# Second layer computed unturned, with a float16 feed-forward and its ELU split between ScalarE and VectorE

## The reference, cut to what matters

```
h = elu(_gat_heads(enc_inputs, adj, W_heads, a_heads))      # layer 1, four heads
h = transpose(h, (0, 2, 1, 3)).reshape(B, N, -1)
out = _gat_heads(h, adj, W_out[None], a_out[None])[:, 0]     # layer 2
out = elu(out)
ffn = maximum(out @ w1 + b1, 0.0) @ w2 + b2
y = ffn + out
return (y - mean(y)) / sqrt(var(y) + LN_EPS) * ln_gamma + ln_beta
```

## Time and profile before

| | |
|---|---|
| median of 3 runs | 1723.54 us (1720.91 to 1724.05) |
| span of the profiled execution | 1722.6 us |
| TensorE busy | 1584.4 us, 92% |
| VectorE busy | 1452.3 us, 84% |
| ScalarE busy | 1382.1 us, 80% |
| GpSimd busy | 1004.7 us, 58% |
| DMA moved | 242.45 MB, mean 141 GB/s |

### The profile page before, as it was taken

The page is one execution under the profiler, slowest core; times in us unless marked ns, Lnnn a source line. Parts: engine busy times, 40 slices in busy tenths (PEclk is TensorE's granted clock), DMA queues, the critical chain, the costliest instruction groups (busy, mean ns, idle before and its releaser), DMA issues.

```text
span 1722.6 us, 36184 instructions
## 1 busy us (share of the span) xinstructions
PE 1584.4 (92%) x13119; PEld 1319.3 (77%) x13120; DVE 1452.3 (84%) x2520; ACT 1382.1 (80%) x1858; POOL 1004.7 (58%) x1425
## 2 busy tenths in 40 slices
PE   5548999999999999999999999999999999999965
PEld 3336878788787887788887887888777888888854
DVE  5877699879998899979999799988999798898583
ACT  4177499879988799878997799878997799999660
POOL 4064367447575566656575566656666475675271
PEclk9769999999999999999999999999999999999988
DMA  8266499749986698678977699868976698798572
GB/s 262 57 147 115 94 190 162 120 95 189 174 151 117 123 187 164 118 122 160 189 141 117 113 184 178 137 98 152 190 156 112 104 172 172 129 133 147 101 118 36
DMA packets 780882, 242.45 MB, mean 141 GB/s; under 512 B 746368, under 2 KB 774016, under 8 KB 780576
## 3 DMA queue, kind: packets, MB, share of 16 engines
q1 hardware_dynamic: 771744, 231.70, 72.1%
q0 software_dynamic: 8960, 8.42, 4.3%
HBM read 38.54 MB, written 16.94 MB: 32 GB/s over the span
## 4 chain that ended last, share of the span: by engine, by line
PE 49%; DVE 18%; ACT 13%; issue 10%; DMA 5%; POOL 3%; SPq 1%; DVEq 0%; ACTq 0%; POOLq 0%
PE ps L129 11%; PE ps L1260 7%; PE ps L1261 7%; PE ps L1266 7%; DVE p_lo L1041 5%; PE ps L138 5%; PE ps L1280 4%; PE ps L1293 3%; ACT p_hi L925 3%; ACT xr L912 3%; DVE xr L1034 3%; PE ps L1341 2%; DMA cat<-f_rows 2%; ACT xr L918 2%; DVE ht_lo L1066 2%
## 5 line engine op out<-in xcount | busy, mean ns | idle before, releaser
L1260 PE MATMUL ps<-pt_hi,hv_hi 128*128 128x256 f16 x2048 | 463.8, 274 | 26.4 <-DMA pt_hi<-p_hi 26.4
L1261 PE MATMUL ps<-pt_hi,hv_lo 128*128 128x256 f16 x2048 | 463.7, 274 | 0.0
L1041 DVE SCALAR_TENSOR_TENSOR p_lo<-xr,rden,p_hi 128x1024 f16<-128x1024 f32 x320 | 409.6, 1280 | 30.4 <-ACT p_hi L925 30.4
L925 ACT ACTIVATE p_hi<-xr,rden 128x1024 f16<-128x1024 f32 x320 | 365.4, 1142 | 32.8 <-POOL rden L849 32.8
L847 POOL TENSOR_SCALAR den<-sums 128x1 f32<-128x1 f32 x320 | 156.4, 489 | 363.2 <-ACT xr L918 361.2
L918 ACT ACTIVATE xr<-xr,shift 128x1024 f32<-128x1024 f32 x320 | 365.5, 1142 | 2.4 <-POOL shift L862 2.4
L1034 DVE CUSTOM_DVE_ANT_0 xr<-cat,mask_add 128x1024 f32<-128x1024 f32 x256 | 311.2, 1217 | 7.5 <-DMA cat<-f_rows 7.5
L912 ACT ACTIVATE xr<-xr,f1h 128x1024 f32<-128x1024 f32 x256 | 292.6, 1143 | 5.5 <-DVE mx L1034 5.5
L849 POOL TENSOR_TENSOR rden<-den,minus_one 128x1 f32<-128x1 f32 x320 | 268.3, 838 | 26.7
L860 POOL TENSOR_SCALAR zt<-mx,f1h 128x1 f32<-128x1 f32 x256 | 197.6, 772 | 120.0 <-DVE mx L1034 117.1
L1266 PE MATMUL ps<-pt_lo,hv_hi 128*128 128x256 f16 x2048 | 266.3, 273 | 0.9 <-DMA pt_lo<-p_lo 0.9
(11 more groups left out here) (192 smaller groups left out, 3193.3 us busy)
## 6 DMA issues: line engine op xcount, KB each, us to landing
cat<-f_rows SPq DMA_DIRECT2D x32, 512.0 KB, 4.6
out<-xx SPq DMA_DIRECT2D x32, 256.0 KB, 2.4
xx<-in_x SPq DMA_DIRECT2D x28, 256.0 KB, 3.3
out<-fin POOLq DMA_DIRECT2D x28, 256.0 KB, 5.3
pt_hi<-p_hi SPq DMA_TRANSPOSE x320, 3.3
pt_lo<-p_lo SPq DMA_TRANSPOSE x320, 3.3
adj_i<-in_adj SPq DMA_DIRECT2D x4, 1024.0 KB, 11.7
f2o<-f2o_rows SPq DMA_DIRECT2D x8, 512.0 KB, 4.4
```

The source lines that it names most:

```text
L925: nc.scalar.activation(p_hi[:, k % P_SLOTS, :], xr[:, k % X_SLOTS, :], ACT.Copy, scale=rden[:, k % 8:k % 8 + 1]).then_inc(hi_done, 1)
L1041: nc.vector.scalar_tensor_tensor(p_lo[:, k % P_SLOTS, :], xr[:, k % X_SLOTS, :], rden[:, k % 8:k % 8 + 1], p_hi[:, k % P_SLOTS, :], ALU.mu ...
L1260: nc.tensor.matmul(to, vh, hi, start=t == 0, stop=False)
L1261: nc.tensor.matmul(to, vl, hi, start=False, stop=False)
```

## The change

1. **Layer 2 unturned.** In `attend` of a layer-2 pair the turned probabilities are now the stationary operand and the values move, so the output has tokens on partitions. It is still 48 matmuls of 256 columns. The waits are by unit: the matmuls of the first unit start when its own transposes have landed.
2. **ELU of layer 2.** ScalarE does the exponential (`elu_exp`) and then, after `softmax` of the same step, a second operation `elu_below`: maximum of 0 and C - C e, in place, with scale and bias from columns of `sc`. VectorE has one operation left: maximum(x, 0) minus that. The min-and-add operation on VectorE goes for layer 2.
3. **Float16 feed-forward.** `o2_high` (ScalarE, step n-5) and `o2_low` (VectorE, n-6) split the ELU output of each pair into float16 halves of 128 x 512; SyncE's queue turns both (`turn_o2`, n-6) into `hs_hi` and `hs_lo`, shared with the first layer's tasks. `ff1` uses three float16 products per block (12 matmuls of 512 columns per half batch) in place of four float32 matmuls of 512 columns.
4. **Residual and b2.** The ELU output is already in token order, so the identity matmuls go; one bfloat16 matmul per tile adds b2 (`b2_rows`), and `y_out` adds the residual in the same single operation over 1024 columns.
5. **Steps.** `CLOSING` and `LAST` change, part of `STEADY` moves by one step, `GAP` goes from 6 to 8.
6. **Start.** w1 is scaled and split, b2 is split into three bfloat16 rows on GpSimd, with one more norm product.

Cut to its core:

```diff
-        GAP = 6
+        GAP = 8
...
-                      turn_h0_0=-38, turn_h0_1=-34, m0=-31, m1=-30, m2=-29, m3=-28, mj_high0=-31, mj_high1=-29, mj_high2=-28, mj_high3=-27,
...
+                      turn_h0_0=-37, turn_h0_1=-33, m0=-30, m1=-29, m2=-28, m3=-27, mj_high0=-30, mj_high1=-28, mj_high2=-27, mj_high3=-26,
...
-        CLOSING = dict(ff1_0=-1, ff2_0=2, ff1_1=4, ff2_1=6, hidden_0=1, hidden_1=5, y_0=4, y_1=9, save_f2o=-22, load_f2o=-16)
...
+        CLOSING = dict(ff1_0=2, ff2_0=4, ff1_1=6, ff2_1=8, hidden_0=3, hidden_1=7, y_0=5, y_1=9, save_f2o=-22, load_f2o=-16)
...
+            def turn_o2(j):
...
+                cols = slice(i // 4 * N + i % 4 * F, i // 4 * N + (i % 4 + 2) * F)
+                for whole, part, ready in ((hs_hi, o2_hi[:, c % 2, :], o2hi_done), (hs_lo, o2_lo[:, :], o2lo_done)):
+                    sp.wait_ge(ready, c + 1)
+                    sp.dma_start_transpose(whole[:, cols].rearrange("p (t i) -> p t i", i=P), part).then_inc(o2_T[c % 2], DMA)
...
+            def elu_below(j):
+
+                act.wait_ge(e2_done, count2(j) + 1)
+                e = eq[:, j % 2, :, :].rearrange("p k n -> p (k n)")
+                nc.scalar.activation(e, e, ACT.Relu, bias=scale(S_OREC), scale=scale(S_ONEG)).then_inc(exp_done, 1)
...
+            def o2_high(j):
...
+                nc.scalar.activation(o2_hi[:, c % 2, :], o2_of(j), ACT.Copy, scale=2.0 ** -P_LOG).then_inc(o2hi_done, 1)
...
+                    nc.vector.scalar_tensor_tensor(o2_of(j).rearrange("p (k n) -> p k n", k=KF), x, 0.0, e, ALU.max, ALU.subtract).then_inc(elu_done, 1)
...
+                if layer == 2:
+                    for u in range(2):
+                        to = psA[:, (j % 2) * 512 + u * F:(j % 2) * 512 + (u + 1) * F]
+                        pe.wait_ge(hi_T[slot + u], turn)
...
+                for slot in range(2):
+                    pe.wait_ge(o2_T[slot], (2 * p + i + 1) * 2 * DMA)
...
-                    for k in range(KF):
-                        last = nc.tensor.matmul(to[:, t * F + k * P:t * F + (k + 1) * P], o2T_of(p, i)[:, k, tok], ident[:, :], start=False, stop=k == KF - 1)
+                    last = nc.tensor.matmul(to[:, t * F:(t + 1) * F], pick[:, :], b2_rows[:, :], start=False, stop=True)
```

More of the change, by code:

```diff
@@ L158, in scores_T @@
                 for t in range(T):
[L159 removed]
+                    last = nc.tensor.transpose(to[:, t * NF:(t + 1) * NF], rows[:, t * P:(t + 1) * P], ident8[0:NF, 0:NF])
                 return last
@@ L995, in _ @@
                     softmax(unit_at(n + 3))
+                j = pair_at(n - ELU_EXP + 2)
+                if j is not None and kinds[2 * j][0] == 2:
+                    elu_below(j)
                 if unit_at(n + 2) is not None:
@@ L1003, in _ @@
                     ht_high(j)
+                j = pair_at(n - O2_HIGH)
+                if j is not None and kinds[2 * j][0] == 2:
+                    o2_high(j)
                 for s in range(B):
@@ L1187, in _ @@
                     ht_low(j)
+                j = pair_at(n - O2_LOW)
+                if j is not None and kinds[2 * j][0] == 2:
+                    o2_low(j)
                 for s in range(B):
```

148 lines of the change are left out of this document (109 added, 39 removed).

## The result

The changed kernel takes 1784.14 us (median of 4, 1782.91 to 1786.41) against 1723.8 us for the kernel before on the same chip: ratio 1.0353, 95% interval [1.0338, 1.0367]. It is 60 us slower, where 1727.7 was forecast with a range that ended at 1750. Slower was the likeliest of the three outcomes that the prediction gave (0.53), but by 4 us, little more than the 3.4 us that it could tell from no change; the size was missed by far.

A forecast was written before the change was run, and what follows sets the result against it. TensorE was taken to bound layer-1 units, taking turns with ScalarE in layer-2 stretches. Stretches +11.4, end -7.5, start +0.3 gave +4.2 on 1722.6, plus 0.9 to the median: 1727.7 us; own bounds 1718 to 1736, 8-in-10 range 1703 to 1750.

The forecast's parts named there:

- What TensorE saves: In `ff1` and `ff2`: 4.4 us per batch, 35 us over eight batches, if TensorE were the only bound.
- What ScalarE gets: Layer-2 stretch: `elu_below` and `o2_high` add 0.6 us each, 1.2 per pair and 4.8 per stretch.
- What VectorE gets: Per layer-2 pair: a 0.42 us operation goes, a 0.75 us one comes; +0.3, or 10 us in all, mostly beside waits.
- Rival B: Layer-2 stretch: longer ELU chain holds VectorE, ScalarE waits for its masked row; 3 to 4 us more per stretch, 1747; chance 0.20.
- SyncE's queue: Eight new half-size transposes per batch beside 80 full ones hold the next high part at most 0.8 us; costed at nothing.
- The sum of one stretch: Layer-2 stretch and what follows: -0.7 + 1.3 + 0.9 = +1.5 us, +2.7 in the first two; together 11.4.
- the 1.3 per stretch: From pair 156 on, one `ff1` more is still to do, where TensorE is the bound: +1.3 us.
- The 0.9 per stretch: `m0` to `m3` move one step, so two waits of 0.87 us at `m` in place of one: +0.9 us.
- The start: Two more 256-column matmuls in a chain with the norm, other new work beside idle time: +0.3 us.
- C: Clock rival: new TensorE idle pieces in the layer-2 stretch bring slow matmuls behind them; +8 us, 1736; chance 0.08.
- The end: Units 312 to 319: shorter serial chain -4.4, start by unit -2.6, earlier `hidden` -1.7, new ScalarE operations +1.2; sum -7.5 us.
- The 2.6 for a start by unit: At the end, TensorE does half a pair before the second unit's transpose lands instead of waiting: -2.6 us.

The follow-up runs named there:

- g2_tensor_alone: `g1_no_split` with the feed-forward's steps, the last batch's steps and the gap of the kernel before; output not the reference's: 1720.21 us, ratio 0.9979.
- g1_no_split: `e3_front_elu` without `o2_high`, `o2_low` and `turn_o2`, so `ff1` reads leftover buffer contents; output not the reference's: 1735.91 us, ratio 1.0077.
- e3_front_elu: Changed kernel with the first graph layer's steps one earlier and layer 2's ELU as two VectorE operations, without ScalarE's clamp: 1763.11 us, ratio 1.0224.
- e1_front_back: Changed kernel with the first graph layer's steps (turn_h0, m, mj_high, mj_low) put back one step earlier, as in the kernel before: 1769.66 us, ratio 1.0255.
- f3_no_turn: `e1_front_back` without the 32 DMA transposes of the second layer's output; output not the reference's: 1757.09 us, ratio 1.0202.
- g4_before_shift: Kernel before with only the first graph layer's steps (turn_h0, m, mj_high, mj_low) moved one later: 1736.33 us, ratio 1.0077.
- g3_end: `e3_front_elu` with the load of the last batch's second row one step earlier and batch 6's later feed-forward steps earlier: 1761.09 us, ratio 1.0218.
- e4_below_early: Changed kernel with ScalarE's clamp directly behind the exponential, ahead of `rectify` and `softmax`: 1784.80 us, ratio 1.0347.

## Why the prediction was wrong, step by step

**What TensorE saves: right in size.** From its start to the start of the next matmul the second `ff1` of a batch takes 2.59 us and `ff2` 3.90 in the changed trace, as worked out (2.6 and 3.9). TensorE's busy time fell by 9.6 us only, not by the 35 that were named as a sign: in `g2_tensor_alone` it fell by 27.5, and attends at the lower clock give some of it back. **The reason why it doesn't arrive: half right.** The prediction saw ScalarE as the second bound of the stretch and gave the 35 us up. `g2_tensor_alone` shows that the saving is lost, but the engine was VectorE at least as much: 94.3 of 100.9 us over the twenty units, and in `g1_no_split` an operation more per pair costs 2 us on ScalarE and 25 on VectorE. I had read it as "45.05 of 49.40" in the earlier trace rows and dismissed it since "its idle time is mostly waits for ScalarE".

**What ScalarE gets: right.** The clamp is 0.80 us long and `o2_high` 0.62; less the overlap of 0.1 they are 0.7 and 0.5, in sum the 1.2 that was taken. They cost little: some 2 us for all of `o2_high`, 5 to 7 for the clamp. `hidden`, whose row now reads `sc` too, takes 1.43 us where it took 1.25, which the prediction didn't have.

**What VectorE gets: the step that failed.** "+0.3, or 10 us in all, most of it beside waits", and at nothing in the sum: the operation that came was set against the one that went. As busy time that was right (94.35 us after, 94.27 before, over the twenty units). As time of the kernel the exchange isn't even. An operation of `o2_low`'s size and place costs 25 us alone, more than the 19.5 that it lasts, because waits of TensorE grow with it and the attends behind them run slow. The operation that the ELU gave up brought nothing back: with the clamp on ScalarE in its place the kernel is 5 us slower than with both on VectorE (`e3_front_elu` against `e1_front_back`). Why it brings nothing is argued and not shown; ScalarE is then the fuller one between attends 188 and 194. Another place for `o2_low` in VectorE's order was not tried, so load and place are not told apart. Rival B, with 1747 us the nearest, has VectorE hold the stretch too, but by another way: ScalarE would idle for the masked row. In the changed kernel it does so once from the second batch to the gap, for 0.3 us.

**SyncE's queue: right for the periods, wrong for the end.** At nothing it was costed, and `f3_no_turn` shows nothing from attend 44 to 272. At the end the transposes cost 11.5 us, beside waits of VectorE that no sentence of the prediction has: `o2_lo` is a single buffer, so each `o2_low` waits until the transpose before has landed. VectorE waits so four times, all at the end, 21.9 us in total.

**The sum of one stretch: near at its end, wrong behind it.** `hidden_0` ended 38.7 us after the exponential (906.83 less 868.16), inside the forecast 36.6 to 39.0, and pair 156 started 43.3 after, 0.4 above the upper bound of 42.9. But the exponential itself came 12.6 us after attend 144, before 11.3: 1.3 us of the loss lie ahead of the mark, where the sum didn't look. TensorE's new idle time was 7.2 us where 5 was named, and before pairs 148, 150 and 152, not 150, 152 and 154. From attend 156 to 164 the forecast was +1.3 and +0.9; the trace has +5.6 (53.3 against 47.7). The work moved there is the 1.3; most of the rest is waiting. `m1` waits 2.73 us where I took 0.87, because in this kernel VectorE is later with `m_low`, and `w_head` waits 0.80 and 0.26 for `g_low`. Of the two terms the 1.3 per stretch was near: `g1_no_split`, with the later steps and the gap, takes 8.9 us more than `g2_tensor_alone` between attends 64 and 272, six stretches. The 0.9 per stretch, 5 us in all, became 13 alone in the kernel before and 17 with the rest of the change. The waits of 0.87 were taken from the kernel before and are right for it (`g4_before_shift`); they do not hold where the engine that is waited for has fallen behind.

**The start.** +0.3 was forecast, and the profiles show +4.9 ahead of attend 64. 3.2 of it lie between attends 34 and 44, where the shifted steps of the third batch stand; the other 1.7 are within what the start of single executions differs by.

**The clock: the rival that was too small.** C had 0.08 and 8 us for slow matmuls behind two gaps per stretch; the forecast itself had nothing for them. Behind waits of over 1 us, the kernel before has 3 such slow attends from attend 64 on, the changed kernel 9, which at 1.67 us each is 10 of the 60 us. That is C's size, but on top of the waits and not in their place.

**The end: wrong in sign.** From attend 310 to the end of the span: 97.0 us before, 90.5 in `g2_tensor_alone`, so TensorE's part is -6.5 and the -7.5 was near for that. The chain behind attend 318 is 4.4 us shorter there, just as forecast. The 2.6 for a start by unit did not come: from 312 to 318 it is 0.2, since pair 316 then waits for the ELU of pair 312 (5.23 us in the changed kernel) and not for a transpose. So that the two sums lie so near is partly luck. Then 101.1 with the later steps and the gap, 109.8 with the split, 113.2 with the clamp, 111.7 after. "`GAP` of 8 costs nothing, because all engines stand still there" is false for the kernel before (6.4 us), and it was the wrong question for the changed one: steps of `ff1_1` and `ff2_1` further back put `hidden_1` behind the first softmax rows of the last batch, and TensorE waits 9.2 us for it. `g3_end` moves them, and the time stays.

**The last batch's first layer** (attend 264 to 304, +9.9) was in the sum only as one more stretch. `g2_tensor_alone` has 3.7 of it already (attend 272 to 304: 140.4 us, before 136.8). Its cause wasn't settled. Nor was it shown what carries the 11.8 us over the gap into the end, since three edits that moved attend 312 forward by up to 9.6 us gave most or all of it back by attend 318.

**The range.** Its upper end follows from its terms (six times 0.5 and 0.8 are 8 above 1727.7), the lower doesn't: six times 1.9 and 0.8 are 16 below, so 1711.5 and not 1718. The measured time lies far above either.

## What to carry to other kernels

Before you credit an engine's saving, add up every engine's busy time over the same stretch: where two are within a few per cent of each other, the saving of one is worth at most the way down to the other. Here it was less, 3.6 of 35 us, and each microsecond put on the other cost all of itself and more. A step moved by one in a static order is not a small edit: which idle time it falls into matters, and a wait copied from the old trace holds only while the engine that is waited for keeps its lead. The releaser that a row names is the last of those that were late; moving it alone (as `e4_below_early` did) is the cheap way to find that out.
